# Two-layer attention and convolution kernel: ScalarE sums part of each head's softmax denominators from the scores of the maximum pass

## The reference

```python
m = jax.image.resize(mask, (B, 1, H, W), method='bilinear')
q = proj(Wq, bq) / math.sqrt(hd); k = proj(Wk, bk); v = proj(Wv, bv)    # (16, 4096, 32)
attn = jax.nn.softmax(jnp.einsum('bnd,bmd->bnm', q, k), axis=-1)
fuse = jnp.einsum('bnm,bmd->bnd', attn, v)
hybrid = _conv1x1(jnp.concatenate([x, fuse], axis=1), Wf, bf)
x = hybrid * m + x * (1.0 - m)
# second layer: edge = relu(bn(dwconv3x3(x))); gate from the means of x;
# 1x1 conv of [x * gate, edge], bn, dwconv3x3, 1x1 conv, bn, times x
```

## Time and profile before

| | us |
|---|---|
| median of 3 runs | 4120.01 (4120.0 to 4120.87) |
| the profiled execution | 4121.6 |
| its span | 4119.8 |
| PE busy | 3956.2 (96%) |
| POOL busy | 3263.9 (79%) |
| DVE busy | 2992.0 (73%) |
| ACT busy | 2377.2 (58%) |
| attention, first block of the maximum pass to last denominators copied | 240.9 to 3652.3 |

### The profile page before, as it was taken

The page is one execution under the profiler, slowest core; times in us unless marked ns, Lnnn a source line. Parts: engine busy times, 40 slices in busy tenths (PEclk is TensorE's granted clock), DMA queues, the critical chain, the costliest instruction groups (busy, mean ns, idle before and its releaser), DMA issues. The chain is left out here.

```text
span 4119.8 us, 82469 instructions
## 1 busy us (share of the span) xinstructions
PE 3956.2 (96%) x20853; PEld 2046.8 (50%) x20853; DVE 2992.0 (73%) x5094; ACT 2377.2 (58%) x4488; POOL 3263.9 (79%) x1488
## 2 busy tenths in 40 slices
PE   7979999999999999999999999999999999959797
PEld 4535555555555555555555555555555555424343
DVE  3257777777777777777777777777777777518989
ACT  1216666666666666666666666666666666621213
POOL 3428999999999999999999999999999999940000
PEclk9959999999999999999999999999999999979898
DMA  6941110111011101110111011101110000022021
GB/s 199 283 116 40 39 24 22 30 39 31 22 33 42 31 19 32 42 32 22 31 42 32 22 33 42 31 22 32 42 32 22 22 22 21 10 58 76 26 77 41
DMA packets 223398, 188.86 MB, mean 46 GB/s; under 512 B 124434, under 2 KB 149188, under 8 KB 222916
## 3 DMA queue, kind: packets, MB, share of 16 engines
q1 hardware_dynamic: 223108, 185.67, 16.9%
HBM read 124.06 MB, written 61.21 MB: 45 GB/s over the span
## 5 line engine op out<-in xcount | busy, mean ns | idle before, releaser
L831 DVE TENSOR_REDUCE block_max<-mx 128x1 f32<-128x512 f32 x4096 | 2513.7, 681 | 798.6 <-PE mx L657 788.9
L786 ACT ACTIVATE prob<-st 128x512 f32<-128x512 f32 x4096 | 2140.4, 607 | 1152.9 <-PE st L650 1141.0
L505 POOL TENSOR_TENSOR prob_sum<-prob_sum,prob 128x1024 f32<-128x1024 f32 x768 | 1819.6, 2386 | 10.3 <-PE acc L689 10.2
L650 PE MATMUL st<-queries,keys 97*128 97x512 f32 x4096 | 1589.9, 410 | 5.4 <-issue 2.9
L657 PE MATMUL mx<-keys,max_queries 96*128 96x512 f32 x4096 | 1557.5, 412 | 27.3 <-DMA keys<-k_scratch 27.2
L505 POOL TENSOR_TENSOR prob_sum<-prob 128x1024 f32<-128x1024 f32 x512 | 1220.2, 2383 | 224.4 <-PE acc L689 162.9
L650 PEld LDWEIGHTS st<-queries,keys 97*128 97x128 f32 x4096 | 768.5, 189 | 611.4 <-ACT prob L786 352.7
L669 PE MATMUL acc<-prob,values 128*32 128x512 f32 x8192 | 1000.2, 600 | 0.0
L657 PEld LDWEIGHTS mx<-keys,max_queries 96*128 96x128 f32 x4096 | 781.8, 192 | 374.1 <-issue 134.0
L669 PEld LDWEIGHTS acc<-prob,values 128*32 128x32 f32 x8192 | 207.5, 109 | 449.5 <-issue 260.4
L689 PE MATMUL acc<-prob_sum,ones 128*32 128x512 f32 x2048 | 234.8, 599 | 5.3 <-ACT num_part L761 4.7
(11 more groups left out here) (106 smaller groups left out, 1193.8 us busy)
## 6 DMA issues: line engine op xcount, KB each, us to landing
max_queries<-q_scratch SPq DMA_DIRECT2D x384, 64.0 KB, 1.9
queries<-q_scratch SPq DMA_DIRECT2D x384, 64.0 KB, 1.9
keys<-k_scratch SPq DMA_DIRECT2D x168, 128.0 KB, 2.5
x<-in_x SPq DMA_DIRECT2D x18, 512.0 KB, 4.3
q_scratch<-high SPq DMA_DIRECT2D x32, 256.0 KB, 4.3
k_scratch<-high SPq DMA_DIRECT2D x16, 512.0 KB, 4.9
q_scratch<-low SPq DMA_DIRECT2D x32, 256.0 KB, 5.1
k_scratch<-low SPq DMA_DIRECT2D x16, 512.0 KB, 4.9
```

The source lines that it names most:

```text
L505: nc.gpsimd.tensor_tensor(psum[k][:, :, :], a, prob[:, (first + i) % RING, :, :], ALU.add).then_inc(added[False], 1)
L650: nc.tensor.matmul(st[bank(i, p)][:, :], kk[gp][:, h, s * P:(s + 1) * P], qq[p][:, h, :], start=True, stop=True).then_inc(scores, 1)
L786: nc.scalar.activation(prob[:, s % RING, h, :], st[bank(i, p)][:, :], ACT.Exp).then_inc(exp_done, 1)
L831: nc.vector.tensor_reduce(bmax[p][:, j // MB, j % MB:j % MB + 1], mx[j % MAX_BANKS][:, :], AX.X, ALU.max).then_inc(mx_taken, 1)
```

## The change

ACT computes, for each group, the exponentials of the maximum pass's last two blocks (the last 1024 of the 4096 keys; 128 queries x 1024) with the negated maximum as bias, and its accumulator output gives their sum per query (`tail_sum`). The exponentials themselves (`tail_exp`) aren't used. These 8 key tiles leave the denominators' other path: POOL has 6 chains of 4 (18 additions), and PE has 3 "S". For that the negated maximum is made group by group: DVE reduces six blocks of 512 and then the last two in one instruction of 1024, and then the 7 columns at once. The two banks of the last blocks are free when ACT has read them, not when DVE has (`max_block` waits for `tail_summed`). The eight instructions stand in ACT's order after the exponentials in `TAIL_AFTER`. SP stores the sums to DRAM with one DMA of 128x8 single elements per unit, behind the row's DMAs, and `normalize` reads three parts and not two. `ORDER` is another, with 3 "S" and 23 scores ahead; the copies, the inversion and POOL's scaling stand elsewhere.

```diff
-GROUPS = [4, 4, 4, 4, 4, 4, 2, 2]
+GROUPS = [4, 4, 4, 4, 4, 4]
-PLAIN = MT - sum(GROUPS)
+TAIL = 2
+SUMMED = MT - TAIL * NSUB
+PLAIN = SUMMED - sum(GROUPS)
+HN = 2 * NSUB
+TAKES = MB - TAIL + 1
-ORDER = ("ssmmmsmsVsmsmsmmsmsmsVsmssmmsmsmmssmVsmsmsmsmsmsmsmsVVsmsmsmsmsmsmsmsmsVVms"
-         "mssmmmsmsmVsmsmsmsmmsmssVVVmssmsmmsmsmsmsVVVVmsmsmsmsmsmmssmsmVmmsmssSSSSSS")
-SCORES_AHEAD = 18
+ORDER = ("msmVVVmssmsmmsmsmsmsmsVVsmsmsmsmsmsmsmsmsVVsmsmsmsmsmsmsmsmsVVmsmsmsmsmsm"
+         "smsmsVVVsmmssmmsmsmsVsssmmVmsmsmsmsmmssmVVsmsmsmssmmmssmmSSSmsmsmssmmsmsms")
+SCORES_AHEAD = 23
-INVERT = 61
+INVERT = 57
-NUM_AFTER, DEN_AFTER = 14, 18
-SCALE_AFTER = 17
+NUM_AFTER, DEN_AFTER = 12, 15
+SCALE_AFTER = 12
+TAIL_AHEAD = 0
+TAIL_AFTER = [0, 8, 15, 23, 30, 39, 48, 57]
+TAIL_FIRST = BLOCKS_AHEAD // MB
...
             def row(u, p):
-                sp.wait_ge(nmax_ready, u + 1)
+                sp.wait_ge(nmax_ready, HN * (u + 1))
...
+                tail = scratch["den"][bass.ds(u, 1), 4 * CH:6 * CH]
+                sp.wait_ge(tail_summed, HN * (u + 1))
+                sp.dma_start(tail.rearrange("a (i n) -> n (a i)", n=P), part[p][:, :],
+                             allow_slow_non_contiguous=True).then_inc(part_stored, 16)
...
-            def max_block(v, p, gp, j):
-                pe.wait_ge(mx_taken, MAXMM * v + j + 1)
+            def max_block(v, p, gp, j, first=False):
+                last, older = (j - MAX_BANKS) // MB, (j - MAX_BANKS) % MB
+                if older < MB - TAIL:
+                    pe.wait_ge(mx_taken, TAKES * HN * v + (TAKES * (last + 1) + older + 1))
+                elif j >= MB or not first:
+                    pe.wait_ge(tail_summed, HN * v + (last + 1))
...
+            def sum_tail(v, p, hn, first=False):
+                if hn == 0 and not first:
+                    act.wait_ge(part_stored, 16 * v)
+                if hn or not first:
+                    act.wait_ge(tail_summed, HN * v + hn)
+                act.wait_ge(nmax_ready, HN * v + hn + 1)
+                nc.scalar.activation(tail_exp[:, :, :], mx[:, MAX_BANKS - TAIL:MAX_BANKS, :], ACT.Exp,
+                                     bias=nmax[p][:, hn:hn + 1].bitcast(F32),
+                                     accum_out=part[p][:, hn:hn + 1]).then_inc(tail_summed, 1)
...
+            for n in range(HN + TAIL_FIRST):
+                sum_tail(n // HN, n // HN, n % HN, first=n < HN)
             unit(0, 0, prev=False)
...
                 for j in range(MAXMM):
-                    dve.wait_ge(mx_ready, MAXMM * v + j + 1)
-                    nc.vector.tensor_reduce(bmax[p][:, j // MB, j % MB:j % MB + 1], mx[j % MAX_BANKS][:, :], AX.X,
-                                            ALU.max).then_inc(mx_taken, 1)
+                    hn, blk = j // MB, j % MB
+                    if blk < MB - TAIL or blk == MB - 1:
+                        k = min(blk, MB - TAIL)
+                        banks = mx[:, blk % MAX_BANKS - blk + k:blk % MAX_BANKS + 1, :]
+                        dve.wait_ge(mx_ready, MAXMM * v + j + 1)
+                        nc.vector.tensor_reduce(bmax[p][:, hn, k:k + 1], banks.rearrange("p b n -> p (b n)"), AX.X,
+                                                ALU.max, negate=True).then_inc(mx_taken, 1)
+                    if blk == MB - 1:
+                        dve.wait_ge(mx_taken, TAKES * (HN * v + hn + 2))
+                        nc.vector.tensor_reduce(nmax[p][:, hn:hn + 1], bmax[p][:, hn, :], AX.X,
+                                                ALU.min).then_inc(nmax_ready, 1)
                     between(v, j, prev, older)
-                dve.wait_ge(mx_taken, MAXMM * v + MAXMM + MAX_BANKS)
-                dve.wait_ge(row_loaded, ROW_INC * (v + 1))
-                nc.vector.tensor_reduce(nmax[:, :], bmax[p][:, :, :], AX.X, ALU.max, negate=True).then_inc(nmax_ready, 1)
```

More of the change, by code:

```diff
@@ L441, in attention_phase @@
         ones = sb("ones", [P, HD])
-        bmax = [sb(f"block_max{p}", [P, 2 * NSUB, MB]) for p in range(2)]
-        nmax = sb("negated_max", [P, 2 * NSUB], F32R)
+        bmax = [sb(f"block_max{p}", [P, HN, TAKES]) for p in range(2)]
+        nmax = [sb(f"negated_max{p}", [P, HN], F32R) for p in range(2)]
+        tail_exp = sb("tail_exp", [P, TAIL, CH])
+        part = [sb(f"tail_sum{p}", [P, HN]) for p in range(2)]
         warm = sb("exp_warm", [P, 1])
@@ L452, in attention_phase @@
         st = [ctx.enter_context(nc.psum_tensor(f"st{i}", [P, CH], F32)) for i in range(BANKS)]
-        mx = [ctx.enter_context(nc.psum_tensor(f"mx{i}", [P, CH], F32)) for i in range(MAX_BANKS)]
+        mx = ctx.enter_context(nc.psum_tensor("mx", [P, MAX_BANKS, CH], F32))
         acc = ctx.enter_context(nc.psum_tensor("acc", [P, CH], F32))
@@ L469, in attention_phase @@
         nmax_ready = sem("negated_max_ready")
+        tail_summed = sem("tail_summed")
+        part_stored = sem("tail_sum_stored")
         row_loaded = sem("max_row_loaded")
@@ L562, in normalize @@
                 sp.wait_ge(den_ready, v + 2)
-                sp.dma_start(row.rearrange("a (i n) -> (a i) n", i=4), den[0:P:HD, :]).then_inc(den_stored, 16)
+                sp.dma_start(row[:, 0:4 * CH].rearrange("a (i n) -> (a i) n", i=4), den[0:P:HD, :]).then_inc(den_stored, 16)
                 sp.wait_ge(den_stored, 16 * (v + 2))
-                sp.dma_start(dcol[:, :, :], row.rearrange("a (e p k) -> (a p) e k", e=2, p=P)).then_inc(dcol_loaded, 16)
+                sp.wait_ge(part_stored, 16 * (v + 2))
+                sp.dma_start(dcol[:, :, :], row.rearrange("a (e p k) -> (a p) e k", e=3, p=P)).then_inc(dcol_loaded, 16)
                 sp.wait_ge(rcol_ready, v + 1)
@@ L737, in _ @@
                     pe.wait_ge(kv_loaded[0], KV_INC)
-                max_block(0, 0, 0, j)
+                max_block(0, 0, 0, j, first=True)
             pe.wait_ge(qm_loaded[1], Q_INC)
@@ L744, in _ @@
             pe.wait_ge(q_loaded[0], Q_INC)
-            pe.wait_ge(row_loaded, ROW_INC * 2)
+            pe.wait_ge(row_loaded, ROW_INC)
             for i in range(SCORES_AHEAD):
@@ L776, in buffer_free, with unit @@
                     act.wait_ge(added[own], ADDS[own] * v + adds_until(k, i))
-                else:
+                elif t < SUMMED:
                     act.wait_ge(sums_done, SUMS * v + (len(GROUPS) + t - GROUP_END[-1]) // 2 + 1)
-            def unit(u, p, prev=True):
+            def sum_tail(v, p, hn, first=False):
[7 more added lines that the diff above has]
+                                     accum_out=part[p][:, hn:hn + 1]).then_inc(tail_summed, 1)
+            def unit(u, p, prev=True, ahead=2):
                 for i in range(TILES):
@@ L786, in unit @@
                     nc.scalar.activation(prob[:, s % RING, h, :], st[bank(i, p)][:, :], ACT.Exp).then_inc(exp_done, 1)
+                    for x, at in enumerate(TAIL_AFTER):
+                        d, hn = divmod(TAIL_AHEAD + x, HN)
+                        if i == at and d < ahead and (prev or TAIL_AHEAD + x >= TAIL_FIRST):
+                            sum_tail(u + 1 + d, (p + 1 + d) % 2, hn)
                     if prev and i == NUM_AFTER:
@@ L795, in _ @@
             nc.scalar.activation(warm[:, :], ones[:, 0:1], ACT.Exp)
+            for n in range(HN + TAIL_FIRST):
+                sum_tail(n // HN, n // HN, n % HN, first=n < HN)
             unit(0, 0, prev=False)
-            with act.Fori(0, UNITS // 2 - 1) as u2:
+            with act.Fori(0, UNITS // 2 - 2) as u2:
                 unit(u2 * 2 + 1, 1)
                 unit(u2 * 2 + 2, 0)
-            unit(UNITS - 1, 1)
+            unit(UNITS - 3, 1)
+            unit(UNITS - 2, 0, ahead=1)
+            unit(UNITS - 1, 1, ahead=0)
             copy_num(UNITS - 1)
@@ L805, in _ @@
         def _(dve):
-            dve.sem_inc(mx_taken, MAX_BANKS)
+            dve.sem_inc(mx_taken, TAKES)
             if PIECES:
@@ L822, in between @@
                         invert(v - 2)
-                for at, piece in zip(ADD_AFTER, PIECES):
+                for at, piece in zip([], PIECES):
                     if prev and j == at:
```

15 lines of the change are left out of this document (8 added, 7 removed).

## The result

The changed kernel takes 4378.25 us (median of 4 runs, 4377.67 to 4380.74) against 4120.32 before: the ratio is 1.0627, with a 95% interval of 1.0609 to 1.0645. It is 6% slower, where 3971 us had been forecast. The span of the profiled execution is 4378.9 us. All times here are medians of executions in the chip's usual state; two slow ones, 7284.07 us of the kernel before and 11287.52 us of e12, are left out.

The account below looks back on a forecast made before the run. PE's work was taken as the bound: a unit falls 2.53 us to 49.75, times 62 is -157, the ends -11.3, the start +17.5, together -151 from 4121.6 to 3971 us; range 3944 to 4030.

Parts of the forecast that it names:

- the one on SP: SP's queue: issuing the sums' store takes 0.5 to 5.0 us, and nothing behind it is late.
- The rival on SP's queue: The store holds SP over 15 us, so normalization and next row are late; about 4280 us at 20 us, chance 0.02.
- the mark for it: Sign of a wrong prediction in the changed profile: SP's issue of the store above 10 us.
- the marks of being wrong: PE waiting on `tail_sum` in every group, SP's issue of the store above 10 us, or granted clock below 1.00.
- the loops' own cost: PE's wait per unit in the kernel before, about 0.1 us, carried over unchanged as 0.11.
- The row: Row DMAs for the next unit's score 0: chain 8.46 us against 8.30 available, so PE waits 0.2 to 0.3 per unit.
- The quiet unit: Length of an attention unit after the change: 49.39 + 0.25 + 0.1 = 49.75 us, 2.53 less.
- The ends: Units 62 and 63 with what follows the last addition: -11.3 us; the start: +17.5 us.
- Three "S" and a run less: PE's removed work per unit: three "S" 2.57 us and one run 0.32, together 2.89.
- The chain through the banks: Block 7 to next group's block 2: 3.30 us needed, distances 3.44 to 4.53; waits of 0.05 to 0.1 us.
- POOL was not the bound: Rival that the work goes but nothing is won because POOL is the real bound; chance 0.01.
- the rival of dearer sums: ACT's sum costs more than 1.25 us; at 1.6 the kernel takes 4018 to 4050 us, chance 0.23.

Follow-up runs that it names:

- e12: The changed kernel with the sums' store as 1024 single elements 64 bytes apart in DRAM and a second DMA gathering the columns; 4047.01 us.
- e4: The kernel before, plus 1024 constants per unit moved as single elements to a row in SBUF by 8 DMAs; 4120.28 us.
- e3: The kernel before, plus a store of 1024 single elements per unit to an unused DRAM row, behind the row's DMAs; 4305.86 us.
- e1: The changed kernel with the sums' store written as 128 runs of 32 bytes, output values wrong; 4041.09 us.
- e9: The kernel of e6 with SP's eight row DMAs released one by one, each by its own group's maximum; 4007.90 us.
- e2: The changed kernel with the sums taken by 8 DMAs to a row in SBUF and from there to DRAM in one run; 4045.16 us.
- e6: The kernel of e2 with four units in ACT's loop body and not two; 4031.08 us.
- e7: The kernel of e3 with half the elements, 512 single elements written to DRAM; 4291.94 us.
- e11: The kernel of e3 with an eighth of the elements, 128 single elements written to DRAM; 4205.19 us.
- e8: The kernel of e3 with the store issued some 25 us earlier in the unit, behind the load of the denominators' columns; 4128.52 us.

## Why the prediction was wrong, by its own steps

**The step that failed is the one on SP**: "Nothing is late." It priced the store by the time that it holds SP, 0.5 to 5.0 us, and SP took 0.44 for it. What it holds is not SP but the transfers behind it, among them the instructions of engines that no semaphore ties to it: a packet of instructions behind it took up to 7.8 us, where the longest before took 1.4, and ACT stood 203.9 us in 31 waits. The rival on SP's queue (4280 us, chance 0.02) put the danger at the right DMA, but took the place to be SP's issue and wanted four times the row's rate; the mark for it, an issue of the store above 10 us, never came (the longest was 1.1). Of the marks of being wrong, it was the granted clock below 1.00 that came: 0.95 over the attention. The row's DMAs were taken as the nearest rows for its price. They are single elements too, but they end in SBUF: e4 shows that these cost nothing, e3 that those to DRAM, side by side, cost 186 us. The Trainium skill's rule on single elements was named and left without a price.

Size of this step: 4378 less e1's 4041, 337 us.

**The other 70 us** (4041 against 3971) are terms that were missed or mis-sized:
- The jump back. I carried 0.11 a unit as "the loops' own cost", from a kernel in which ACT had 17 us of idle time a unit to hide it (2193.69 busy of 3289.70 us). In the changed kernel ACT has 7, and the sum behind the first exponential holds banks that PE wants. It costs 1.1 in every second unit, some 33 us, and at PE's outer loop's two jumps back units of 57 to 58 us where 53.8 stood before, some 10 more.
- The row: 0.25 a unit forecast, 0.2 to 0.3 in most rows of PE's wait but 0.40 on average in e1 (24.2 us in 60); e9 gains 23 us by removing it.
- The quiet unit: 49.75 forecast, 50.05 to 50.1 measured in e1 and e2, and 49.8 in e9, where 49.5 would have followed. PE's wait for the copy of the numerators, 0.18 in each unit, is about half of the 0.3; the rest isn't accounted for.
- The ends: the last two units fall from 97.9 to 93.1 us, 4.9, where I had 11.3; what bounds them now wasn't settled. The start cost less than forecast: the first copy of the denominators is at 372.5 in e1 against 362.6, +9.9, and +17.5 had been summed (the copy also stands three exponentials earlier in ACT's order).

Two slips in the working changed nothing in the sum: a "V" or an "S" is 8 matmuls in the rows, not four, and POOL had 2.7 us a unit to spare before, not 4.5.

**What held.** Three "S" and a run less were to give 2.89 a unit on PE. Units fell by 2.2 from 52.28 to 50.1, and the waits above for the row and the numerators hide 0.4 more; the last 0.3 isn't shown. The chain through the banks was right to a tenth: the sum takes 1.12 us, and its accumulator is read out by an instruction of its own of 0.2 us.

```profile
L806 ACT ACTIVATE tail_exp<-mx,negated_max 128x1024 f32<-128x1024 f32 x512 | 574.0, 1121 | 106.7 <-DVE negated_max L879 87.5 <-issue 7.9
L806 ACT ACTIVATION_READ_ACCUMULATOR tail_exp<-mx,negated_max 128x1 f32 x512 | 104.8, 205 | 0.0
```

1.12 less the overlap plus 0.2 is 1.2 from start to end, where 1.25 had been taken. At the start the groups follow each other at 6.0 us, forecast 5.9:

```profile
244.17 1.11 ACT L806 ACTIVATE tail_exp<-mx,negated_max 128x1024 f32<-128x1024 f32 x1 [18.02 <-DVE negated_max L879]
...
250.17 1.11 ACT L806 ACTIVATE tail_exp<-mx,negated_max 128x1024 f32<-128x1024 f32 x1 [4.80 <-DVE negated_max L879]
```

POOL was not the bound, the rival of dearer sums didn't come, and the idea of the change was sound: with its sums stored another way it is worth 1.7 to 1.8% (e12 and e2), and 2.7% with e6 and e9.

## What to carry to other kernels

A DMA is priced twice: by what it holds of its own queue, and by what it does to everything else that moves at that time, above all where it writes single elements of several partitions side by side into DRAM; there write runs, go by way of SBUF, or spread the elements. The packets of kind "instruction" in the trace show whether the fetching of instructions was held. When a trace shows a wait without a releaser at a loop's jump back, look at which transfers were issued in the 10 us before. And a cost that the old kernel hides under idle time of an engine isn't a cost of zero once the change fills that engine.

## What the runs showed of the hardware that I had not expected

- 1024 elements of 4 bytes to DRAM, side by side and from 128 partitions, hold up other transfers, among them those of instructions, for up to about 10 us (store at 2103.24, ACT on again at 2113.50 in e3). ACT's waits without a releaser last 8.2 us on average with 1024 elements (e3), 7.4 with 512 (e7) and 5.2 with 128 (e11). With 64 bytes from one to the next, 1024 cost nothing that can be measured (4119.37 against 4118.04), nor do they in SBUF (e4).
- The same store costs 11 us or 186, depending on whether ACT's loop jumps back within the next 10 us (e8 and e3). A packet of instructions of 8 KB took up to 8.0 us behind the store in e3, and 0.3 to 0.7 in the kernel before.
- A jump back of a loop whose body fills two units costs ACT about 1.1 us even with quiet queues (e2), 0.9 of which go with the jump (e6).
- The granted clock fell to 1.2 GHz within a wait of PE of 6.5 us and stayed there for 6.6 us after it.
